# Two stages of graph attention: the order of attention times values, and where the big tiles start

## The reference

```
y   = adj @ x[b];  z = y @ W0 + b0                      # layer 0
u   = layernorm(x + z)
qkv = u @ Wqkv;    8 heads of 64                        # layer 1
attn = softmax(q k^T / 8, masked where adj == 0)
o   = (attn @ v) @ Wproj + bproj
out = layernorm(u + o + (layernorm(o) * gamma + beta))
```

## Time and profile before

| | |
|---|---|
| Time, median of 3 runs | 3717.84 us (3716.96 to 3719.47) |
| Profiled execution: time, span | 3719.2 us, 3717.4 us |
| PE, busy share of the span | 97% |
| DVE | 77% |
| ACT | 58% |
| POOL | 41% |
| PE waiting for pt_lo ahead of L756 | 34.8 us in 61 waits |
| DMA, share of the 16 engines | 24.8% |

### The profile page before, as it was taken

One profiled execution on the slowest core, in us unless ns is written; L12 is line 12 of the kernel. 1 busy time (PEld: TensorE's weight loads), 2 busy tenths in 40 slices (PEclk: granted clock), 3 DMA queues, 4 the chain that ended last, 5 costly groups with the idle time before them and its releaser, 6 DMA issues.

```text
span 3717.4 us, 64437 instructions
## 1 busy us (share of the span) xinstructions
PE 3600.8 (97%) x18960; PEld 2879.1 (77%) x18960; DVE 2878.2 (77%) x6681; ACT 2140.3 (58%) x4505; POOL 1538.6 (41%) x2311
## 2 busy tenths in 40 slices
PE   8999999989999999999999999999999999999996
PEld 6888888867777777777777777777777777777775
DVE  7666666646888888888888888888888888888887
ACT  4343444436666666666666666666666666666664
POOL 4555555522333333334333333333343333333334
PEclk9999999999999999999999999999999999999998
DMA  6555555531111111111111111111111111111110
GB/s 195 178 181 181 181 181 178 175 101 37 56 45 45 45 45 45 45 45 45 45 46 50 45 45 51 45 45 45 51 45 45 47 49 45 45 45 45 47 55 32
DMA packets 344957, 276.18 MB, mean 74 GB/s; under 512 B 13664, under 2 KB 275808, under 8 KB 344928
## 3 DMA queue, kind: packets, MB, share of 16 engines
q1 hardware_dynamic: 344928, 275.83, 24.8%
HBM read 141.56 MB, written 134.22 MB: 74 GB/s over the span
## 4 chain that ended last, share of the span: by engine, by line
PE 34%; issue 21%; POOL 16%; DVE 6%; ACT 1%; POOLq 0%; DVEq 0%
PE bank L789 10%; POOL probs L670 9%; PE bank L807 6%; PE bank L737 5%; PE bank L726 4%; POOL t L686 4%; PE bank L756 4%; PE bank L757 3%; POOL o_rstd L676 2%; DVE o_stats L969 1%; DVE pt_lo L943 1%; PE bank L773 1%; DVE probs L929 1%; POOL probs L667 1%; DVE o L986 1%
## 5 line engine op out<-in xcount | busy, mean ns | idle before, releaser
L843 ACT ACTIVATE probs<-probs,bias_row 128x512 f32<-128x512 f32 x1024 | 730.5, 715 | 643.9 <-DVE bias_row L929 643.9
L943 DVE TENSOR_TENSOR pt_lo<-bank,pt_hi 128x512 fp32r<-128x512 f32 x1024 | 667.5, 683 | 111.7 <-ACT pt_hi L851 102.1
L670 POOL TENSOR_SCALAR probs<-probs,inv_sums 128x480 f32<-128x480 f32 (+1 forms) x1024 | 688.5, 686 | 0.0
L929 DVE CUSTOM_DVE_ANT_0 probs<-bank,mask_bias 128x512 f32<-128x512 f32 x1024 | 661.0, 682 | 0.0
L851 ACT ACTIVATE pt_hi<-bank 128x512 fp32r<-128x512 f32 x1024 | 555.9, 596 | 166.5 <-PE bank L737 162.7
L667 POOL TENSOR_TENSOR probs<-probs,inv_sums 128x32 f32<-128x32 f32 x512 | 123.6, 241 | 1274.7 <-DVE inv_sums L935 1271.0
L737 PE MATMUL bank<-ident,probs 128*128 128x128 f32 x4096 | 535.7, 274 | 17.7 <-POOL probs L670 15.2
L737 PEld LDWEIGHTS bank<-ident,probs 128*128 128x128 f32 x4096 | 480.1, 141 | 90.7 <-POOL probs L670 22.7
L756 PE MATMUL bank<-pt_hi,v 128*128 128x512 f32 x1024 | 414.9, 405 | 37.5 <-DVE pt_lo L943 34.8
L773 PE MATMUL bank<-x_hi,w_hi 128*128 128x512 f32 x1024 | 411.4, 402 | 28.6 <-DVE ot L961 17.2
L773 PE MATMUL bank<-x_hi,w_lo 128*128 128x512 f32 x1024 | 417.3, 407 | 0.0
(11 more groups left out here) (90 smaller groups left out, 7651.7 us busy)
## 6 DMA issues: line engine op xcount, KB each, us to landing
x_in<-in_x_dram SPq DMA_DIRECT2D x32, 1024.0 KB, 5.6
ut_hi<-ut_hi_sb SPq DMA_DIRECT2D x128, 256.0 KB, 3.7
ut_lo<-ut_lo_sb SPq DMA_DIRECT2D x128, 256.0 KB, 3.7
u_beta_rows<-ub SPq DMA_DIRECT2D x32, 1024.0 KB, 4.4
x_hi<-ut_hi SPq DMA_DIRECT2D x128, 256.0 KB, 4.3
x_lo<-ut_lo SPq DMA_DIRECT2D x128, 256.0 KB, 4.6
out_dram<-o SPq DMA_DIRECT2D x128, 256.0 KB, 3.1
ub_row<-u_beta_rows SPq DMA_DIRECT2D x124, 256.0 KB, 2.9
```

Source lines behind the costliest of these rows:

```text
L670: pool.tensor_scalar(probs[:, k % 2, a, cols], probs[:, k % 2, a, cols], inv_sums[:, k % 4, a:a + 1], 0.0, ALU.mult, ALU.add)\
L843: act.activation(probs[:, k % 2, a, :], probs[:, k % 2, a, :], ACT.Exp, bias=bias_row[:, k % 4, a:a + 1], scale=-1.0, accum_out=sums[:, k ...
L929: dve.tensor_tensor_reduce(probs[:, k % 2, a, :], s_bank[k % 2][a][:], mask_bias[:, k % T, :], -SCALE, 3.0e38, ALU.add, ALU.min, bias_row[ ...
L943: dve.tensor_tensor(pt_lo[:, a, :, cols], t_bank[a][:].rearrange("p (m n) -> p m n", m=T), f32(pt_hi[:, a, :, cols]), ALU.subtract).then_i ...
```

## The change

There are two edits. ident and half_neg are allocated from the other end of SBUF, so that nothing stands between mask_bias and bproj_row. Every tile declared after them moves down by 544 bytes, and the big ones start 128 past a multiple of 2048, as w_hi, w_lo and mask_bias do. ident itself now starts at byte 228832, 1504 past a multiple of 2048.

In `attend_v` a head waits for pt_hi (pthi_made) at first, issues its four products with pt_hi, waits for ptlo_made, and issues the four with pt_lo. The number of products is the same. The four v tiles are loaded as weights in the order 0, 1, 2, 3, 0, 1, 2, 3 and no longer 0, 0, 1, 1, 2, 2, 3, 3.

```diff
         mask_bias = keep("mask_bias", [P, T, N], BF16)
-        ident = keep("ident", [P, P], F32)
-        half_neg = keep("half_neg", [P, 1], F32)
         bproj_row = keep("bproj_row", [P, D], F32)
         gamma_row = keep("gamma_row", [P, D], F32)
+
+
+        ident = whole.enter_context(nc.sbuf_tensor("ident", [P, P], F32, side="right"))
+        half_neg = whole.enter_context(nc.sbuf_tensor("half_neg", [P, 1], F32, side="right"))
...
                     def attend_v(b, p, last_part, more):
                         for a in range(2):
-                            pe.wait_ge(ptlo_made, b * 32 + (8 * p + 7 + a))
+                            pe.wait_ge(pthi_made, b * 32 + (8 * p + 7 + a))
...
-                            for m in range(T):
-                                w = v[:, m, 2 * p + a, :, :].rearrange("p s d -> p (s d)")
-                                pe.matmul(o_bank[a][:], w, pt_hi[:, a, m, :], start=m == 0, stop=False)
-                                last = pe.matmul(o_bank[a][:], w, pt_lo[:, a, m, :], start=False, stop=m == T - 1)
+
+                            for part in (pt_hi, pt_lo):
+                                if part is pt_lo:
+                                    pe.wait_ge(ptlo_made, b * 32 + (8 * p + 7 + a))
+                                for m in range(T):
+                                    w = v[:, m, 2 * p + a, :, :].rearrange("p s d -> p (s d)")
+                                    last = pe.matmul(o_bank[a][:], w, part[:, a, m, :],
+                                                     start=part is pt_hi and m == 0, stop=part is pt_lo and m == T - 1)
                             last.then_inc(pv_done, 1)
```

## The result

The changed kernel takes 3677.55 us (median of 4 runs, 3676.94 to 3677.95) against 3717.61 (3716.96 to 3719.47) before on the same chip: ratio 0.9891 (0.9879 to 0.9903), 40 us less. The forecast was 3677.

The account below looks back on a forecast made before the run. PE's instruction stream was taken to bound both layers. Waits and pace gave 1.28 us a batch, x 31 = 39.7, plus 0.9 around it, 40.6 us off 3717.84: 3677 us, range 3664 to 3700.

Parts of the forecast that it names:

- The waits: PE's pt_lo stalls before attend_v's first products, 1.36 us a batch; 0.72 to count, 22.3 us in all.
- what is late next: qk after groups 2 and 3 needs DVE's ot sum, so PE comes forward 0.28 us there, not 0.60.
- The pace: qk, V and projection products fall from 233 to 227 ns with equal operand starts; 0.56 us a batch counts.
- Equal modulo 512 is fast: Weights and moving data with starts equal modulo 512 run at 227 ns; 32 bytes off, at 233.
- The 144 products outside the steady batches: 96 qk products and the last 48 of the projection, each 6.4 ns faster: 0.9 us.
- What the prediction took as nothing: Moved tiles' effect on transposes (6.6 us either way possible), DVE, ACT and POOL operations (19 us possible) and DMA: none.
- The new waits ahead of the products: PE's waits for DVE's ot sum before the first products of two groups grow by 0.3 us each.
- the first pt_lo would be ready: In attend_v, pt_lo done near 2049.1, fifth product's weight load at 2049.41: hidden, 0.3 us in hand less 0.1 for the signal.
- That placement does nothing: Rival: the slow pace belongs to w's tiles, only the waits gain, 22.3 us: 3695 us; chance 0.19.
- That a multiple of 64 costs: Rival: tiles starting on 64 bytes are slow, every product goes at 233.3 ns: 3719 us, no change; chance 0.07.
- That equal starts at 128 collide: Rival: every pair starting at 128 slows to 240 ns: 3774 us; chance 0.05.
- That DVE swallows the pace too: Rival: DVE falls behind, PE's lead goes into ot waits, group 0 too; 0.3 us a batch, 3708 us; chance 0.09.

Follow-up runs that it names:

- order alone: Kernel before the change with only the new attend_v order, no tile moved: 3695.12 us, ratio 0.9936 against the kernel before.
- placement on top: Changed kernel against the kernel with only the new attend_v order, so the tile moves added to it: 3695.12 to 3677.55 us, 17.6 us.
- the placement kernel: Changed kernel with the old attend_v order, so only the tiles moved against the kernel before: 3704.7 us, ratio 0.9962.
- the last kernel: Changed kernel with LayerNorm's second addition on DVE covering 64 of 512 columns, part of the result left out: 3646.12 us, ratio 0.9804 against the kernel before.
- the three moves: Changed kernel with DVE's LayerNorm additions in steps 5, 8, 10, 13: 3680.02 us; row 0's put behind next step's ot sums: 3686.25; rows 0 and 2: 3715.31.

## Why the prediction was right

**The waits.** All of the 1.36 us of stalls left attend_v (1.34 in the steps). Only 0.28 was to count at groups 2 and 3. In the table a group is cut where its effect ends, after the stretch of 20 that follows it:

| effect of group (its steps) | forecast: wait, pace | order alone | placement on top | both |
|---|---|---|---|---|
| 0 (1 to 4) | 0.16, 0.22 | 0.14 | 0.22 | 0.36 |
| 1 (5 to 8) | 0, 0.14 | 0.00 | 0.13 | 0.12 |
| 2 (9 to 12) | 0.28, 0.10 | 0.29 | 0.10 | 0.39 |
| 3 (13 to 0) | 0.28, 0.10 | 0.27 | 0.09 | 0.36 |
| batch, us | 0.72, 0.56 | 0.71 | 0.54 | 1.25 |

The waits alone were put at 3695, the order alone took 3695.12. The step that carried this was the look at what is late next: with PE's stalls counted in full, the forecast would have been 0.64 a batch too low, 20 us. Its reason for these two groups was short by a link. It found ACT busy with its exp and followed DVE's rows back; the chain that decides goes from DVE's o_shift over ACT, and at group 3, which was taken to be like group 2, DVE itself is idle for 1.69 us ahead of the sum. The number holds, for on this chain too no row after pt_lo of step 9 (step 13 for group 3) is seen to wait for PE.

**The pace.** The read of the earlier trace rows, that the relation of the two starts sets 227 or 233, held: 32 bytes put back between w and the rest bring the 233.3 back (3695.88), and moving everything together changes nothing. The rule in the Trainium skill ("TensorE: Matmul & The Clock Gate", "Step-by-step: what each phase is for") that the load has its own port and takes nothing from the running product would give 3695; the runs at 233.3 and 226.9 ns disagree with it here, though they don't say where the two accesses meet. "Equal modulo 512 is fast" was wrong in its size: 256 apart is as fast. It touched no number, because the change makes the starts equal. The 144 products outside the steady batches were put at 0.9 us; 40.1 less 38.8 leaves 1.3 for all that lies outside. What the prediction took as nothing was nothing: the transposes went from 108.9 to 108.8 ns, DVE's pt_lo from 683 to 684, its minimum (L929, now L935) from 682 to 684, ACT's exp stayed at 715, and the DMA share at 0.55 and 0.16. That forecast and time meet within a microsecond is luck in part: the order's 0.71 and the placement's 0.54 a batch had been put at 0.72 and 0.56, and the 1.3 outside the batches at 0.9, so that the errors cancel.

**Its own small errors.** The new waits ahead of the products were put at 0.3 and came to 0.39 each: the 0.12 of pace that the sum itself let go into waiting belongs to them as well. That the first pt_lo would be ready some 0.2 us before the weight load of the fifth product held: in step 11 it ended at 2031.97 and the load began at 2032.21, and steps 3, 11 and 15 last 6.33 us like step 7, which never had the stall.

**The rivals.** That placement does nothing: refuted by the placement kernel and the 17.6 us. That a multiple of 64 costs: z stayed at 227.0 at place 128. That equal starts at 128 collide: the same number. That DVE swallows the pace too: group 0 gave its 0.22. DVE's load is real nevertheless. The waits for its sum at groups 3 and 0, where ACT's half of ot comes last behind DVE's o_shift, take back 0.67 of the 1.34 us, and the last kernel buys 31 us with less work on DVE, which none of the three moves did.

## What to carry to other kernels

Give weights and moving data starts that are equal modulo 256 bytes (0 and 256 apart were measured); here two small tiles that fill 544 bytes between them cost 6.4 of 227 ns on every such product. When a stall of the leading engine goes, follow the next engine's rows back to where the leader last led it, and count only what lies ahead of that. Follow the chain over every engine that it crosses: at two of three places here it went from DVE over ACT back to DVE, and at step 12 the work of DVE right ahead of the wait stood beside that chain and was worth nothing. The three kernels that moved DVE's work ended some waits and made others as long or longer; 0.47 us less work at each of four places gave 0.90 us a batch.

## What was not expected of the hardware

The distance from start to start of 512-column products, each with its own weight load, depends on the low bits of the two starts: 226.7 to 227.2 ns at 0 or 256 apart (modulo 512), 233.3 at 32 apart, 232.1 to 232.8 at 128, and at 64 either 233.3 or 229.2, by which of the two is the weights. The 128-column transposes show none of it (108.8 to 109.0). Which part of the chip the two accesses share, and why 64 bytes differ by direction, stays open; distances between 128 and 256 were not tried.
